# A recommender forward pass on one core: the pair products regrouped in three sets of features, and a new order around two lots and layer 0

## What is computed

```python
bot_out = _mlp(dense_x, [bw0, bw1, bw2], [bb0, bb1, bb2])          # 13 -> 512 -> 256 -> 128
gathered = jnp.stack([emb[t][sparse_x[:, t]] for t in range(26)], axis=1)
features = jnp.concatenate([bot_out[:, None, :], gathered], axis=1) # 27 features of 128
Z = jnp.einsum('bnd,bmd->bnm', features, features)
interact = Z[:, LI, LJ]                                             # the 351 pairs i > j
x = jnp.concatenate([bot_out, interact], axis=1)                    # 479
return _mlp(x, [tw0, ..., tw4], [tb0, ..., tb4])                    # 1024, 1024, 512, 256, 1, all with relu
```

## Time and profile before

| what | us |
|---|---|
| median of 3 runs | 214.62 |
| lowest and highest | 210.69 and 214.96 |
| span of the profiled execution, first to last instruction | 179.6 |
| median run less that span | 35.0 |
| TensorE busy in the span | 167.0 (93%) |
| GpSimd busy | 100.7 (56%) |
| VectorE, ScalarE busy | 82.2, 66.3 |

### The profile page before, as it was taken

One profiled execution on the slowest core, in us unless ns is written; L12 is line 12 of the kernel. 1 busy time (PEld: TensorE's weight loads), 2 busy tenths in 40 slices (PEclk: granted clock), 3 DMA queues, 4 the chain that ended last, 5 costly groups with the idle time before them and its releaser, 6 DMA issues.

```text
span 179.6 us, 3315 instructions
## 1 busy us (share of the span) xinstructions
PE 167.0 (93%) x1354; PEld 128.6 (72%) x1354; DVE 82.2 (46%) x177; ACT 66.3 (37%) x103; POOL 100.7 (56%) x112
## 2 busy tenths in 40 slices
PE   1999999899599994999999999989999999999993
PEld 1335557568377783798878889977888898788992
DVE  3202588955165756374452346343506625411422
ACT  0576748664143655133033253112504611110211
POOL 3777776777777777777777777767772000000000
PEclk9999999999999999799999999999999999999999
DMA  4999972434499733242232244422223120000000
GB/s 97 369 337 391 390 239 58 100 66 89 89 302 374 285 79 86 54 100 68 44 61 51 52 105 85 93 46 62 46 59 72 24 53 7 4 0 0 0 0 4
DMA packets 10124, 19.93 MB, mean 111 GB/s; under 512 B 5639, under 2 KB 5771, under 8 KB 9981
## 3 DMA queue, kind: packets, MB, share of 16 engines
q1 hardware_dynamic: 6636, 12.89, 22.0%
q0 software_dynamic: 3328, 6.82, 16.7%
q10 hardware_dynamic: 144, 0.00, 0.0%
HBM read 18.26 MB, written 1.44 MB: 110 GB/s over the span
## 4 chain that ended last, share of the span: by engine, by line
PE 71%; DMA 10%; POOL 8%; issue 4%; SPq 2%; DVE 2%; ACT 2%; POOLq 0%; DVEq 0%; ACTq 0%
PE acc L799 14%; PE acc L803 13%; PE acc L800 12%; POOL rows L420 8%; PE feat L781 6%; PE turned L944 5%; PE feat L763 5%; DMA rows<-in_emb,index 3%; PE turned L881 3%; DMA pairs<-pair_scratch 3%; DMA pair_scratch<-dots 3%; PE acc L829 2%; PE acc L938 2%; PE feat L938 2%; DMA v<-in_bw 1%
## 5 line engine op out<-in xcount | busy, mean ns | idle before, releaser
L420 POOL DMA_INDIRECT rows<-in_emb,index x104 | 99.5, 957 | 34.4 <-issue 30.0
L799 PE MATMUL acc<-w1h,y_split 128*128 128x512 f32 x64 | 27.9, 436 | 0.0
L803 PE MATMUL acc<-w1h,y_split 128*128 128x512 f32 x64 | 26.1, 407 | 0.0
L800 PE MATMUL acc<-w1l,y_split 128*128 128x512 f32 x64 | 25.5, 399 | 0.0
L444 ACT COPY featT<-feat 128x512 f32<-128x512 f32 x16 | 17.6, 1097 | 14.4 <-PE feat L763 14.3
L457 ACT ACTIVATE y_split<-turned 128x512 fp32r<-128x512 f32 x16 | 9.7, 606 | 35.1 <-PE turned L881 35.1
L651 DVE SCALAR_TENSOR_TENSOR y_split<-turned,y_split 128x512 fp32r<-128x512 f32 x16 | 11.1, 692 | 18.7 <-ACT y_split L457 18.7
L799 PE MATMUL acc<-w2h,y_split 128*128 128x256 f32 x64 | 18.8, 294 | 0.0
L803 PE MATMUL acc<-w2h,y_split 128*128 128x256 f32 x64 | 18.0, 281 | 0.0
L763 PE MATMUL feat<-ident,rows 128*128 128x128 f32 x104 | 15.3, 277 | 2.7 <-DMA rows<-in_emb,index 2.7
L800 PE MATMUL acc<-w2l,y_split 128*128 128x256 f32 x64 | 17.8, 279 | 0.0
(11 more groups left out here) (107 smaller groups left out, 255.6 us busy)
## 6 DMA issues: line engine op xcount, KB each, us to landing
w1r<-in_w SPq DMA_DIRECT2D x8, 512.0 KB, 13.8
w2r<-in_w SPq DMA_DIRECT2D x4, 512.0 KB, 6.0
rows<-in_emb,index POOLq DMA_INDIRECT x104, 3.0
w0r<-in_w_pairs SPq DMA_DIRECT2D x3, 512.0 KB, 7.8
top<-in_top_rows SPq DMA_DIRECT2D x1, 1024.0 KB, 12.1
pair_scratch<-dots SPq DMA_DIRECT2D x8, 104.0 KB, 2.3
pair_scratch<-dots SPq DMA_DIRECT2D x8, 71.5 KB
v<-in_bw SPq DMA_DIRECT2D x1, 512.0 KB, 3.6
```

The costliest lines, as they stand in the source:

```text
L420: pool.indirect_dma_start(rows[:, i, :], None, table, bass.IndirectOffsetOnAxis(ap=index[:, c, i:i + 1], axis=0)).then_inc(s_gather[LOTS * ...
L799: nc.tensor.matmul(dst, ah, wh, start=first, stop=False)
L800: nc.tensor.matmul(dst, ah, wl, start=False, stop=False)
L803: return nc.tensor.matmul(dst, al, wh, start=False, stop=end)
```

## The change

Five things, which the diff shows below.

1. The pairs are grouped otherwise. The features are three sets, 11, 11 and 5. Tile 0 is the second set against the first (121 rows). Tile 1 is the first two sets against the third (110 rows) and the third against itself (16 rows). Both are rectangles of `dots`, so they go from SBUF to SBUF in one DMA each, without the scratch buffer. Tile 2 holds the pairs inside the first and inside the second set (110 rows and the bias row), and still goes by the scratch buffer. Rows that hold a pair twice or a square get zero weights. `dots` has 27 columns instead of 26.
2. The DMA of tile 0 is issued by ScalarE, behind its share of `dots_out`, once VectorE's share is there (`across_out`). SyncE issues the rest.
3. Layer 0 goes by tiles: tile 0 for both halves of the columns, then layer 3 of the chunk before, then tiles 1 and 2. ScalarE and VectorE take the second half of layer 2's output ahead of tile 1.
4. In chunk 0 the last two blocks of layer 1 and the first four blocks of layer 2 (half 0), then two of half 1, stand around the last two lots, ahead of the products. ScalarE and VectorE follow suit.
5. The filler before chunk 1's first lot falls from 11 matmuls to 8, and 5 are new at the end of chunk 0.

The diff, cut to its core:

```diff
+SET = 11
+LAST = FEATS - 2 * SET
+HOPS = (SET - 1) // 2
+SET_COLS = SET - 1
 PAIR_TILES = 3
-TILE_FEATS = FEATS // PAIR_TILES
-PAIR_ROWS = TILE_FEATS * HOPS
-COLS = FEATS - 1
-FIRST_ROWS = 16
+PAIR_ROWS = [SET * SET, 2 * SET * LAST + (LAST - 1) * (LAST - 1), 2 * SET * HOPS]
+TILE_ROWS = [PAIR_ROWS[0], PAIR_ROWS[1], PAIR_ROWS[2] + 1]
+PINS = [16, 32, 32]
...
+        def across_out(eng, c, h):
+
+            eng.wait_ge(s_za, HALVES * c + h + 1)
+            eng.wait_ge(s_zd, HALVES * c + h + 1)
+            after(eng, s_xlp, PAIR_TILES * c)
+            eng.dma_start(pair_rows(h, 0, 0, PAIR_ROWS[0]), products(h, SET, SET, 0, SET)).then_inc(s_pin[h][0], 16)
...
+            def pairs_back(c, h):
 
                 sp.wait_ge(s_za, HALVES * c + h + 1)
                 sp.wait_ge(s_zd, HALVES * c + h + 1)
-                for i in range(PAIR_TILES):
-                    after(sp, s_pin[h][i], (16 if i < PAIR_TILES - 1 else 32) * c)
-                low, mid = HALF * h, HALF * h + FIRST_ROWS
-                sp.dma_start(scratch[h, 0:FIRST_ROWS], dots[low:mid]).then_inc(s_scr0[h], 16)
-                sp.dma_start(scratch[h, FIRST_ROWS:], dots[mid:low + FEATS]).then_inc(s_scr1[h], 16)
-
-            def pairs_of(h, n, feats):
-                return flat(scratch, (h * FEATS * COLS + n * (COLS + 1) + 1) * HALF,
-                            [[(COLS + 1) * HALF, feats], [HALF, HOPS], [1, HALF]])
-
-            def pairs_back(c, h):
-
-                half = slice(h * HALF, (h + 1) * HALF)
+                after(sp, s_pin[h][2], PINS[2] * c)
+                for t in range(2):
+                    sp.dma_start(scratch[h, t], products(h, t * SET, SET, t * SET, SET_COLS)).then_inc(s_scr[h], 16)
                 after(sp, s_xlp, PAIR_TILES * c)
                 if (c, h) == (0, 0):
                     sp.wait_ge(s_one, 1)
-                sp.wait_ge(s_scr0[h], 16 * (c + 1))
-                sp.dma_start(pairs[0:PAIR_ROWS, 0, half], pairs_of(h, 0, TILE_FEATS)).then_inc(s_pin[h][0], 16)
-                sp.wait_ge(s_scr1[h], 16 * (c + 1))
-                sp.dma_start(pairs[0:PAIR_ROWS, 1, half],
-                             pairs_of(h, TILE_FEATS, TILE_FEATS)).then_inc(s_pin[h][1], 16)
-                sp.dma_start(pairs[0:PAIR_ROWS - HOPS, 2, half],
-                             pairs_of(h, 2 * TILE_FEATS, TILE_FEATS - 1)).then_inc(s_pin[h][2], 16)
-                sp.dma_start(pairs[PAIR_ROWS - HOPS:PAIR_ROWS, 2, half],
-                             flat(scratch, (h * FEATS * COLS + (FEATS - 1) * COLS + HOPS) * HALF,
-                                  [[HALF, HOPS], [1, HALF]])).then_inc(s_pin[h][2], 16)
+                both = 2 * SET * LAST
+                sp.dma_start(pair_rows(h, 1, 0, both), products(h, 0, 2 * SET, 2 * SET, LAST)).then_inc(s_pin[h][1], 16)
+                sp.dma_start(pair_rows(h, 1, both, PAIR_ROWS[1] - both),
+                             products(h, 2 * SET, LAST - 1, 2 * SET + 1, LAST - 1)).then_inc(s_pin[h][1], 16)
+                sp.wait_ge(s_scr[h], 32 * (c + 1))
+                base = h * 2 * SET * SET_COLS
+                main = 2 * SET_COLS * HOPS
+                sp.dma_start(pair_rows(h, 2, 0, main),
+                             flat(scratch, (base + 1) * HALF,
+                                  [[SET * HALF, 2 * SET_COLS], [HALF, HOPS], [1, HALF]])).then_inc(s_pin[h][2], 16)
+                sp.dma_start(pair_rows(h, 2, main, 2 * HOPS),
+                             flat(scratch, (base + SET_COLS * SET_COLS + HOPS) * HALF,
+                                  [[SET * SET_COLS * HALF, 2], [HALF, HOPS], [1, HALF]])).then_inc(s_pin[h][2], 16)
...
                 nc.scalar.copy(*dot_quadrant(h, 0))
                 nc.scalar.copy(*dot_quadrant(h, 1)).then_inc(s_za, 1)
+                across_out(act, c, h)
...
                 pairs_hi(c, 0)
-                pairs_hi(c, 1)
                 if c > 0:
                     layer2_out(c - 1, 1)
+                pairs_hi(c, 1)
                 pairs_hi(c, 2)
...
+                    layer2_lo(c - 1, 1)
                 pairs_lo(c, 1)
                 pairs_lo(c, 2)
-                if c > 0:
-                    layer2_lo(c - 1, 1)
...
-            keep_going(turned[0], 11)
+            keep_going(turned[0], 8)
...
+                layer0(c, 1, 0)
+                if c > 0:
+                    layer3(c - 1)
                 layer0(c, 0, 1)
                 layer0(c, 0, 2, end=True)
-                if c > 0:
-                    layer3(c - 1)
-                layer0(c, 1, 0)
...
-                if not end:
+                if c == 0:
+                    layer1(c, 1, 6)
+                    layer1(c, 1, 7)
+                    layer2(c, 0, range(0, 2), hi_ready(1, c, 0))
                     turn_lot(c + 1, 1, 2)
+                    layer2(c, 0, range(2, 4))
                     turn_lot(c + 1, 1, 3)
-                layer1(c, 1, 6)
-                layer1(c, 1, 7)
-                if not end:
+                    pe.wait_ge(s_e[1], 2 * c + 2)
+                    layer2(c, 1, range(0, 2))
                     dots_of(c + 1, 1)
-                layer2(c, 0, range(0, 2), hi_ready(1, c, 0))
-                turn(1, c, 1)
-                layer2(c, 0, range(2, 4))
-                layer2(c, 1, range(0, 4))
+                    turn(1, c, 1)
+                    layer2(c, 1, range(2, 4))
+                else:
+                    if not end:
+                        turn_lot(c + 1, 1, 2)
+                        turn_lot(c + 1, 1, 3)
+                    layer1(c, 1, 6)
+                    layer1(c, 1, 7)
+                    if not end:
+                        dots_of(c + 1, 1)
+                    layer2(c, 0, range(0, 2), hi_ready(1, c, 0))
+                    turn(1, c, 1)
+                    layer2(c, 0, range(2, 4))
+                    layer2(c, 1, range(0, 4))
                 layer2(c, 0, range(4, 8), hi_ready(1, c, 1))
                 layer2(c, 1, range(4, 6))
                 turn2(c, 0)
                 layer2(c, 1, range(6, 8))
+                if c == 0:
+                    keep_going(acc_of(1, 0), 5, w0h[:, 0, :])
```

More of the change, by code:

```diff
@@ L55, in pair_order, with within @@
 def pair_order():
-    tiles = []
-    for i in range(PAIR_TILES):
-        for p in range(PAIR_ROWS):
-            n, h = i * TILE_FEATS + p // HOPS, p % HOPS
-            if n == FEATS - 1:
-                a, b = n, HOPS + h
-            elif n + h + 1 < COLS:
-                a, b = n + h + 1, n
-            else:
-                a, b = n + 1, n + h + 1 - COLS
-            tiles.append((a, b))
-    return tiles
+    def within(base, flat):
+        return base + flat // SET_COLS, base + flat % SET_COLS
+    across = [(SET + n, m) for n in range(SET) for m in range(SET)]
+    last = [(n, 2 * SET + m) for n in range(2 * SET) for m in range(LAST)]
+    last += [(2 * SET + n, 2 * SET + 1 + m) for n in range(LAST - 1) for m in range(LAST - 1)]
+    inside = [within(base, n * SET + 1 + h) for base in (0, SET) for n in range(SET_COLS) for h in range(HOPS)]
+    inside += [within(base, SET_COLS * SET_COLS + HOPS + h) for base in (0, SET) for h in range(HOPS)]
+    return [across, last, inside]
 def pair_weights(w, bias):
     out = np.zeros((PAIR_TILES, P, w.shape[1]), w.dtype)
-    for at, (a, b) in enumerate(pair_order()):
-        out[at // PAIR_ROWS, at % PAIR_ROWS] = w[DIM + a * (a - 1) // 2 + b]
-    out[PAIR_TILES - 1, PAIR_ROWS] = bias
+    placed = set()
+    for i, rows in enumerate(pair_order()):
+        for row, (n, m) in enumerate(rows):
+            a, b = max(n, m), min(n, m)
+            if a != b and (a, b) not in placed:
+                placed.add((a, b))
+                out[i, row] = w[DIM + a * (a - 1) // 2 + b]
+    assert len(placed) == FEATS * (FEATS - 1) // 2
+    out[PAIR_TILES - 1, PAIR_ROWS[PAIR_TILES - 1]] = bias
     return out
@@ L200, in rec_kernel @@
         s_z, s_za, s_zd = map(sem, ("dots_done", "dots_copied_act", "dots_copied_dve"))
-        s_scr0 = [sem(f"scratch{h}_first_written") for h in range(HALVES)]
-        s_scr1 = [sem(f"scratch{h}_rest_written") for h in range(HALVES)]
+        s_scr = [sem(f"scratch{h}_written") for h in range(HALVES)]
         s_pin = [[sem(f"half{h}_pairs{i}_in") for i in range(PAIR_TILES)] for h in range(HALVES)]
@@ L265, in dot_quadrant, with dots_free, products, pair_rows @@
             block_ = feat[QUAD * q:QUAD * q + FEATS, :].rearrange("n (g c) -> n c g", c=GROUP_COLS)
-            return dots[HALF * h:HALF * h + FEATS, :, at:at + GROUPS], block_[:, q * FEATS:q * FEATS + COLS, :]
+            return dots[HALF * h:HALF * h + FEATS, :, at:at + GROUPS], block_[:, q * FEATS:(q + 1) * FEATS, :]
+        def dots_free(eng, c, h):
+            after(eng, s_pin[h][0], PINS[0] * c)
+            after(eng, s_pin[h][1], PINS[1] * c)
+            after(eng, s_scr[h], 32 * c)
+        def products(h, n0, ns, m0, ms):
+            return dots[HALF * h + n0:HALF * h + n0 + ns, m0:m0 + ms, :]
```

(18 more changed lines are left out.)

38 lines of the change are left out of this document (21 added, 17 removed).

## The result

The changed kernel takes 223.2 us (median of 4 runs, 222.43 to 223.49) where the kernel before takes 214.34 (4 runs, 210.69 to 214.96). The ratio is 1.0512, with a 95% interval of 1.045 to 1.0573: slower, and outside the range.

What follows compares the result with a forecast made beforehand. TensorE, busy 93% of 179.6 us, was taken as the bound, with GpSimd's gathers a second clock. The terms left 0.4 us gained, 179.2, plus 35.0 around the span: 214.2 us, range 210.6 to 216.2.

Steps and rivals of the forecast that it cites:

- the 35.0 us that the median run has around the profiled span: In the sum: 35.0 us around the profiled span, added to the forecast span of 179.2 to give 214.2 us.
- GpSimd's queue is a second clock that no edit here makes faster, since none touches it: Gathers: one issued every 1.25 us without waiting after 29.55; of gains ahead of 138.8 us at most 0.8 is kept.
- The slack of 0.75 and 0.78 at lot 3: Lot 3 in chunks 1 and 2: its gather lands 0.75 and 0.78 us before its transpose, capping gains there.
- First hand-over: Chunk 0, 42.8 to 52.1 us: direct DMA takes 2.4 to 2.8 us, layer 0's turn 1.9 us earlier, worth 0.
- Around the last two lots: Chunk 0: layer 1 and 2 matmuls fill the gaps; products start at 72.65, gain 1.98 us, about 1.2 from clock.
- Behind the products: End of chunk 0: waits of 1.6 and 0.5 us, fillers 1.15; chunk 1's layer 0 starts 1.1 us earlier.
- Layer 0 by tiles: Chunks 1 to 3: idle of 0.57 us before each turn; chunks 1 and 3 lose 0.25, chunk 2 gains 0.22.
- A (clock): End of chunk 0: clock falls after idles of 1.6 and 0.5 us; 0.6 us slower, 215.2 us; chance 0.2.
- B (dear issue): ScalarE's DMA issue behind the products: at 2 us each, about 3.4 us slower, 218.0 us; chance 0.04.
- C: Tile 0's direct DMA no faster than two hops, 4.8 us; 0.3 us of waits, 214.5 us; chance 0.08.
- D: Gathers land in 2.0 us instead of 2.9 and ScalarE's issue is cheap; 1.1 us kept, 213.5 us; chance 0.08.
- Two of the working's own signs of being wrong: Wrong if: gathers not every 1.25 us, half clock after 76, ScalarE issue above 1 us, `pairs` waits in chunks 1-3.

## Why the prediction was wrong

**"With the 35.0 us that the median run has around the profiled span."** This is the first step that failed. The span and the time of a profiled execution differ by 1.8 to 2.0 us in every run here. The other 33 us are time inside the span that the profile of before did not contain: it showed the kernel as it runs on one kind of chip, and the times were as on the other. There TensorE is idle 30.7 us of a span instead of 12.6 and busy 179.4 instead of 167.0, at a lower clock. The blocks of products take 31.1 us instead of 13, TensorE waits 6.7 us for ScalarE's copies to `featT`, and the first layer 0 begins at 57.34 instead of 47.66. As a constant in the sum the 35.0 did no harm, since both kernels have it; the harm is in what it hid. The warning was in the table: nothing known takes 35 us of a launch, and 31.1 to 35.4 us is a spread that a fixed overhead has not. All terms of the sum were then priced on an execution in which TensorE never stalls.

**"GpSimd's queue is a second clock that no edit here makes faster, since none touches it."** This is the step that cost most. No edit made it faster; but one touches it and makes it slower. Layer 0 by tiles moves the event for which the fourth gather of a chunk is held. I counted what layer 0's new order costs TensorE, and not who else waits for its halves. The working says that GpSimd waited for nobody behind 29.55, and two rows of the profile of before, on GpSimd's timeline, say otherwise:

```profile
86.86 0.94 POOL L420 DMA_INDIRECT rows<-in_emb,index  x1 [0.68 <-issue]
...
119.94 0.94 POOL L420 DMA_INDIRECT rows<-in_emb,index  x1 [0.69 <-issue]
```

Each is the fourth gather, 0.68 or 0.69 us behind the one before it against 0.30 for its neighbours. So the wait for layer 0 was all but binding there already. The slack of 0.75 and 0.78 at lot 3 is no cover for a delay of 2 to 3 us. On a 213 us chip the hold costs more: blocks 5 and 7 go to 8.1 us, and without that wait 3.1 of the 5.1% are gone.

**First hand-over.** The split of the direct DMA's tile began 2.99 us behind the issue (43.52 to 46.51), against 2.4 to 2.8 for the landing alone; the turn came at 51.07 against 50.2. The gain, 2.1 us against the kernel before on that chip (53.19), is lost to the gathers, as forecast.

**Around the last two lots.** No slice is below full clock there on the 181 us chip, as forecast. The products begin at 73.93 instead of the 72.65 of the sum: the blocks of layer 2 ahead of the lots begin only at 70.59, behind a wait for their split, so lot 3 is turned at 73.02, where the kernel before on that chip turned it at 71.40. Against the kernel before on that chip (73.05) that is a loss of 0.9, where I had a gain of 1.98 over the earlier trace rows; the idle of the earlier trace rows was smaller in that execution, and the order alone measured as nothing (1.0031).

**Behind the products.** ScalarE's issue 0.85 (0.75), the wait for its split 1.71 (1.6), VectorE's 0.22 (0.5), the five fillers on the path 1.18 (1.15). All but VectorE's were sized well. They set in from a later start, so layer 0 of chunk 1 begins at 83.72 and not 82.3. With the DMA issued by SyncE the wait is 0.84.

**Layer 0 by tiles.** 0.51 at each turn against 0.57. Of the rivals, on the 181 us chip A (clock) and B (dear issue) did not come, and C and D were too small to matter. Two of the working's own signs of being wrong stand in the profile of the result: gathers are not issued every 1.25 us, and the clock is short of full in 8 slices behind 76 us. The rival that was missing is the one that the waits of `chunk_pace` would have given: the fourth gather held 2 to 3 us, lot 3 late behind a slack of 0.78, some 2 us slower even where TensorE never stalls, and, with 33 us unexplained in the times, a range open towards slower.

**In sum.** Where the profile of before holds, the change costs 2.1%: 0.9% goes when the gathers are not held, 1.0% with layer 0 in the old order, 1.6% when SyncE issues tile 0's DMA, each undone alone and all acting partly through the same late gathers. The prediction had set these costs against gains that did not come. Where the times were taken it costs 5.1%: 3.1% goes with the held gathers and perhaps 1.5% with the order of chunk 0 and its fillers, each undone alone.

**What stays open.** Why a block of products stalls is not shown. The gaps inside blocks come only while gathers are under way and only on one kind of chip; on the 181 us chip one or two gathers are issued in these blocks too, and they take 1.9 us. It is not that GpSimd waits for the products in itself: in the run of the three sets without pacing TensorE had no such gap from 143.7 to 154.6 us, while GpSimd stood in its wait of 19.80 and issued nothing. The profile puts the gaps down to "issue", so a shortage of instructions at TensorE, data that come late, or a signal that comes late are all rivals, and no run tells them apart. What tells the chips apart was not found either. The three sets alone, with the pacing as before, did not run on a 213 us chip, so what is left there of the 5.1% is not fully assigned. No version beat the kernel before by more than the unchanged kernel did (0.9963).

## What to carry to other kernels

Compare the span of a profile with the time of the run that is to be forecast; if tens of microseconds lie between them, the profile is not of the execution that is timed, and the range has to say so. When an order is changed on one engine, list every semaphore that the moved instructions raise and who waits for each, above all a queue that is held back by hand. A hold on transfers that costs nothing on one chip can be what a quarter of the time hangs on at another, so it is moved along with the event that it names.

## What the runs showed of the hardware

Three chips of one type differed by 18% on one program (181 us on one, 213 on two). Of the 31.4 us between the spans of the kernel before (178.7 and 210.1), 18 lie in TensorE's dense blocks of small matmuls, with gaps of 0.2 to 0.5 and 1.1 to 1.2 us between single ones while gathers are under way. The granted clock falls behind such gaps: in the block of the kernel after that begins at 122.05 it is 1.0 up to 124 us and 0.5 from 126 to 130. Its mean over a span is 0.97 to 1.0 on the one chip, 0.91 to 0.96 on the others with pacing, and 0.81 to 0.83 without. GpSimd's gathers issued as fast as the buffers allow cost nothing on the 181 us chip (1.0004, the kernel before), and the changed kernels took 25 to 28% more than the kernel before on a 213 us chip. A DMA from SBUF to SBUF of 121 rows was in use 3.0 us behind its issue, and the issue took 0.85 us of ScalarE's time.
